# Reordered queues in a fused cross-attention and mixture-of-experts kernel: squares of K on ScalarE, scales ahead of low parts, gathers four blocks ahead

## The reference, cut to what matters

```python
# x: (4, 512, 512)   ctx: (4, 512, 256)
y = layernorm(x)
q = ln(y @ Wq + bq)                       # 16 heads of 32, normalised per head
k, v = ln(ctx_main @ Wk + bk), ctx_main @ Wv + bv          # 496 keys
k_dca, v_dca = split(ctx_dca @ Wkv_dca + bkv_dca)          # 16 keys, k_dca normalised too
x1 = x + (attn(q, k, v) + attn(q, k_dca, v_dca)) @ Wo + bo
h = layernorm(x1)
scores = softmax(h @ gate_w.T)            # 64 experts
top6 = top_k(scores, 6)                   # weights normalised to sum 1
# each expert takes at most 384 rows: gate, up (352 wide), silu, down
out = x1 + sum_of_top6(w_e * swiglu_e(h)) + swiglu_shared(h)   # shared one is 704 wide
```

## Time and profile before

| | us |
|---|---|
| median of three runs | 1766.02 (1765.25 to 1768.4) |
| the profiled execution | 1762.85 |
| its span | 1761.1 |
| TensorE busy in it | 1693.0 (96%) |
| VectorE, ScalarE, GpSimd busy | 1090.3, 1028.3, 757.9 |
| mean granted clock of TensorE | 0.982 |

### The profile page before, as it was taken

One profiled execution on the slowest core, in us unless ns is written; L12 is line 12 of the kernel. 1 busy time (PEld: TensorE's weight loads), 2 busy tenths in 40 slices (PEclk: granted clock), 3 DMA queues, 4 the chain that ended last, 5 costly groups with the idle time before them and its releaser, 6 DMA issues. The chain is left out here.

```text
span 1761.1 us, 35834 instructions
## 1 busy us (share of the span) xinstructions
PE 1693.0 (96%) x11782; PEld 1539.8 (87%) x11782; DVE 1090.3 (62%) x2157; ACT 1028.3 (58%) x1871; POOL 757.9 (43%) x719
## 2 busy tenths in 40 slices
PE   4899999999999999999999999999999999999995
PEld 3588888888888888989999999999999999999984
DVE  7555656777566665443666666666666666666664
ACT  4567766666545553222566666666666666666664
POOL 7513222334223230242245555555555555455554
PEclk8899999999899999999999999999999999999997
DMA  5543433433222532312577777777777777777766
GB/s 189 160 117 91 119 105 97 121 95 98 83 84 79 177 107 87 122 38 86 181 227 232 209 214 226 218 210 223 223 216 205 228 221 213 222 232 206 215 198 212
DMA packets 149083, 289.87 MB, mean 165 GB/s; under 512 B 29199, under 2 KB 66319, under 8 KB 139649
## 3 DMA queue, kind: packets, MB, share of 16 engines
q1 hardware_dynamic: 116112, 238.21, 41.9%
q0 software_dynamic: 32880, 50.51, 13.7%
HBM read 243.73 MB, written 64.52 MB: 175 GB/s over the span
## 5 line engine op out<-in xcount | busy, mean ns | idle before, releaser
L2188 POOL DMA_INDIRECT out<-y,ids_s x128 | 209.9, 1640 | 280.3 <-ACT y L2323 254.8
L2448 PE MATMUL ps<-xt_hi,gu_hi 128*128 128x256 f32 (+1 forms) x1856 | 303.5, 285 | 0.6 <-issue 0.6
L2448 PE MATMUL ps<-xt_lo,gu_hi 128*128 128x256 f32 (+1 forms) x1856 | 289.8, 278 | 0.0
L2448 PE MATMUL ps<-xt_hi,gu_lo 128*128 128x256 f32 (+1 forms) x1856 | 289.2, 278 | 0.0
L2223 DVE TENSOR_TENSOR gu_lo<-raw_gu,gu_hi 128x1408 fp32r<-128x1408 f32 (+2 forms) x132 | 214.6, 1625 | 112.5 <-ACT gu_hi L2220 109.3
L1121 ACT ACTIVATE prob<-ps 128x512 f32<-128x512 f32 x256 | 152.2, 597 | 191.4 <-PE ps L1428 169.6
L2448 PEld LDWEIGHTS ps<-xt_hi,gu_hi 128*128 128x128 f32 (+1 forms) x1856 | 250.6, 181 | 9.0 <-issue 3.0
L2448 PEld LDWEIGHTS ps<-xt_lo,gu_hi 128*128 128x128 f32 (+1 forms) x1856 | 244.4, 181 | 0.0
L2448 PEld LDWEIGHTS ps<-xt_hi,gu_lo 128*128 128x128 f32 (+1 forms) x1856 | 244.2, 181 | 0.0
L2168 POOL DMA_INDIRECT xg<-h_rows,ids_g x128 | 191.6, 1497 | 115.2 <-POOL ids_g L2163 50.6
L2280 ACT ACTIVATE h_hi<-h 128x256 fp32r<-128x256 f32 (+1 forms) x240 | 100.6, 419 | 224.0 <-DVE h L2349 223.4
(11 more groups left out here) (316 smaller groups left out, 3000.3 us busy)
## 6 DMA issues: line engine op xcount, KB each, us to landing
raw_gu<-in_w_gu SPq DMA_DIRECT2D x71, 1408.0 KB, 6.7
raw_d<-in_w_d SPq DMA_DIRECT2D x71, 512.0 KB
raw_d<-in_w_d SPq DMA_DIRECT2D x71, 192.0 KB
qs<-qk_rows SPq DMA_DIRECT2D x192, 64.0 KB, 2.2
ks<-qk_rows SPq DMA_DIRECT2D x192, 64.0 KB, 2.0
xa<-in_x SPq DMA_DIRECT2D x16, 256.0 KB, 3.0
qk_rows<-k_hi SPq DMA_DIRECT2D x16, 256.0 KB, 2.2
qk_rows<-k_lo SPq DMA_DIRECT2D x16, 256.0 KB, 2.5
```

What stands on the lines that cost most here:

```text
L2188: pool.indirect_dma_start(out=out, out_offset=bass.IndirectOffsetOnAxis(B.ids_s[:, p, k:k + 1], 0), in_=B.y[:, p, k, :], in_offset=None, b ...
L2448: last = pe.matmul(gu_banks(it, c)[half], gu_columns(w, it, half, d, c), x[:, x_p, d, 0:W], start=i == 0, stop=i == len(steps) - 1)
```

## The change

- Front, K's squares: ScalarE makes them in the front too, after `xt_high` (steps 1 to 3) or after `turned_full` of Q (steps 4, 5); GpSimd keeps Q's. The front of VectorE does `scales` and `ctx_rest` before `rest` of Q. The joined bias `bd` is done in two halves: the sum with `bv` stays at the beginning of step 3, the subtraction of means moves to its end (`bias_of_dca`), and the numbers of `POOL_SPLIT` follow. Tile 1's rows are turned, rounded and subtracted before tile 0's K product and biases.
- Heads: GpSimd counts after scaling; VectorE's `weighted(n)` before `route_top`, `route_mask` after `scales`, `route_code` into the fourth head before the second maxima, slots and weights after `weighted(n+2)`; TensorE turns K before `third_key` where there is a Q product in the unit, and otherwise after `route_pos`.
- Passage: TensorE weighs the last head first and spreads Wo's halves between the turned tiles; the cuts of the last tiles come before those of the first item.
- Experts: `scatter` copies its indices before it waits; after the last items, third blocks are gathered four ahead, their columns copied one block ahead; SyncE loads the gate and up weights of block b+3 and the down weights of block b+2; ScalarE's `act_d` comes before `results`.

The diff, without two hunks that only adapt final waits and the list of returned functions:

```diff
@@ -207,7 +207,7 @@
         SPLIT = dict(wq0=1, wq1=2, cols=3, wk=4, cd=5, kvd0=6, kvd1=7)
-        POOL_SPLIT = dict(bias=1, wv=2, wd_v=3, wd_k_centred=4, bd=5, wd_k=6, wo=6 + DC)
+        POOL_SPLIT = dict(bias=1, wv=2, wd_v=3, wd_k_centred=4, wd_k=5, bd=6, wo=6 + DC)
@@ -555,7 +555,6 @@
                     pool.tensor_tensor(bd[:, D:2 * D], bd[:, D:2 * D], bv[:], ALU.add)
-                    without_means(bd[:, 0:D].rearrange("p (g d) -> p g d", d=HD), sums_bd[:], H)
@@ -571,12 +570,14 @@
-            def squares(j, v, sq, given, summed, done, dca):
+            def bias_of_dca(s):
+                if s == 3:
+                    without_means(bd[:, 0:D].rearrange("p (g d) -> p g d", d=HD), sums_bd[:], H)
+
+            def squares(j, v, sq, given, summed, done):
                 if not tile(j):
...
                 pool.wait_ge(given.sem, given.value(j, 1))
-                if dca and j % T == T - 1:
-                    pool.wait_ge(kd_in.sem, kd_in.value(j // T, 16))
                 if j >= 1:
@@ -588,13 +589,13 @@
             def front(s):
-                squares(s - 2, kb, sq_k, k_bias, k_sum, k_sq, True)
                 weights_first(s)
...
                 weights_then(s)
-                squares(s - 1, qb, sq_q, q_bias, q_sum, q_sq, False)
+                squares(s - 1, qb, sq_q, q_bias, q_sum, q_sq)
                 k_rest(s - 2)
+                bias_of_dca(s)
@@ -620,9 +621,9 @@
-                counted_on(u - 6)
                 scaled(u + 5, kb, H, k_sum, kn_ready)
                 scaled(u + 5, qb, 0, q_sum, qn_ready)
+                counted_on(u - 6)
                 biased(u + 6, P, qb, bq, q_raw, q_bias)
@@ -913,17 +914,19 @@
                     summed(s - 2, sq_k, H, k_sq, k_sum)
+                    scales(s - 7)
+                    ctx_rest(s - 1)
                     if s < 6:
                         rest(s - 3, q_full, q_hi, q_lo, q_high, q_low, q_out)
-                    ctx_rest(s - 1)
-                    scales(s - 7)
                     front_dca(s)
                 j = s - 1
+                if s == 1:
+                    xt_rest(s, FX)
                 taken(j, P, qb, front_q(j), bq, q_ready, trq_ready, q_raw, q_bias)
                 taken(j, keys_of(j), kb, front_k(j), bk, k_ready, trk_ready, k_raw, k_bias)
-                if s < 6:
+                if 1 < s < 6:
                     xt_rest(s, FX)
-                else:
+                if s == 6:
                     summed(s - 1, sq_q, 0, q_sq, q_sum)
@@ -948,33 +951,33 @@
                 maxima(n + 2, 1)
+                weighted(n)
                 route_top(u - 6)
-                weighted(n)
-                route_mask(u - 6)
...
                 scales(u)
+                route_mask(u - 6)
                 maxima(n + 3, 1)
...
                 weighted(n + 1)
-                route_code(u - 6)
...
                 rest(u + 5, k_full, k_hi, k_lo, k_high, k_low, k_out)
+                route_code(u - 6)
+                maxima(n + 4, 1)
+                weighted(n + 2)
                 route_slots(u - 6)
-                maxima(n + 4, 1)
                 route_weights(u - 6)
-                weighted(n + 2)
                 summed(u + 6, sq_q, 0, q_sq, q_sum)
...
             weighted(HEADS - 1)
+            at_rest(WAIT1 + 1)
             residual(WAIT1)
+            at_rest(WAIT1 + 2)
             net.cut_x(dve, item, 0, False)
             net.cut_x(dve, item, 1, False)
-            at_rest(WAIT1 + 1)
-            at_rest(WAIT1 + 2)
             net.cut_gu(dve, item, 0, False)
@@ -1270,6 +1273,7 @@
                 normal(1)
+                xt_high(1, FX)
                 act.wait_ge(wv_in, WV_IN)
@@ -1280,7 +1284,7 @@
                 if s == 1:
-                    xt_high(1, FX)
+                    squares(0, kb, sq_k, k_bias, k_sum, k_sq, True)
                     return
@@ -1293,7 +1297,11 @@
                     xt_high(s, FX)
+                if s < 4:
+                    squares(s - 1, kb, sq_k, k_bias, k_sum, k_sq, True)
                 turned_full(s - 2, FQ_T, trq_ready, q_full, 0, False, q_low)
+                if 4 <= s < 6:
+                    squares(s - 1, kb, sq_k, k_bias, k_sum, k_sq, True)
                 if s == 2:
@@ -1347,10 +1355,10 @@
             item = net.item
+            at_high(WAIT1 + 1)
+            at_high(WAIT1 + 2)
             net.cut_x(act, item, 0, True)
             net.cut_x(act, item, 1, True)
-            at_high(WAIT1 + 1)
-            at_high(WAIT1 + 2)
             net.cut_gu(act, item, 0, True)
@@ -1666,10 +1674,13 @@
                     front_v(s - 3)
+                if s == 1:
+                    front_x(s)
                 if s < 6:
...
                     front_k_product(s - 1)
-                    front_x(s)
+                    if s > 1:
+                        front_x(s)
                     front_q_turned(s - 2)
@@ -1712,9 +1723,12 @@
                 half1(n + 2)
+                if tile(u + 6):
+                    k_turned(u + 5)
+                third_key(n + 2)
                 route_pos(u - 6)
-                k_turned(u + 5)
-                third_key(n + 2)
+                if not tile(u + 6):
+                    k_turned(u + 5)
                 fourth_key(n + 2)
@@ -1725,16 +1739,6 @@
-            item = net.item
-            pe.wait_ge(at_lo.sem, at_lo.value(WAIT1, 1))
-            pe.wait_ge(h2T_in.sem, h2T_in.value(WAIT1 - 1, 1))
-            wo_half(WAIT1, 0)
-            weigh(HEADS - 1, 0)
-            weigh(HEADS - 1, 1)
-            wo_half(WAIT1, 1)
-            weigh(HEADS - 1, 2)
-            weigh(HEADS - 1, 3)
-
             def a_last(j, free, use):
@@ -1746,12 +1750,19 @@
+            item = net.item
+            for t in range(T):
+                weigh(HEADS - 1, t)
+            pe.wait_ge(at_lo.sem, at_lo.value(WAIT1, 1))
+            pe.wait_ge(h2T_in.sem, h2T_in.value(WAIT1 - 1, 1))
+            wo_half(WAIT1, 0)
+            a_last(WAIT1 + 1, v_ready, TILES - 1)
+            wo_half(WAIT1, 1)
+            pe.wait_ge(nmT_in.sem, nmT_in.value(HEADS - 1, 1))
+            a_last(WAIT1 + 2, pos_taken, GROUP1 - 1)
             pe.wait_ge(nmax_ready.sem, nmax_ready.value(HEADS - 1, 2))
...
             net.transpose_chunk(pe, item, 1)
-            a_last(WAIT1 + 1, v_ready, TILES - 1)
-            pe.wait_ge(nmT_in.sem, nmT_in.value(HEADS - 1, 1))
-            a_last(WAIT1 + 2, pos_taken, GROUP1 - 1)
             wo_last(WAIT1 + 1, pv_taken, HEADS - 1)
@@ -2175,12 +2186,12 @@
         p = it.half
+        pool.tensor_copy(B.ids_s[:, p, 0:nb], slots_of(it, B.ids)).then_inc(s_copied.sem, 1)
         if it.known and it.e == SH_ITEMS:
...
             pool.wait_ge(added.sem, added.value(it.expert - 1, 16 * nb))
-        pool.tensor_copy(B.ids_s[:, p, 0:nb], slots_of(it, B.ids)).then_inc(s_copied.sem, 1)
         pool.wait_ge(y_taken.sem, y_taken.value(it.rows, nb))
@@ -2196,10 +2207,14 @@
                 thirds["gather_first"](pool, (it + 2).e - ITEMS)
+            if not (it + 1).exists:
+                thirds["gather_first"](pool, 2)
             scatter(pool, it - 1)
...
         def after(it):
-            thirds["gather_first"](pool, 2)
+            thirds["gather_first"](pool, 3)
+            thirds["weight_column"](pool, FIRST)
+            thirds["row_column"](pool, FIRST)
             scatter(pool, it)
@@ -2328,8 +2343,8 @@
             thirds["act_x"](act, FIRST + 1)
+            thirds["act_d"](act, FIRST)
             results(it)
-            thirds["act_d"](act, FIRST)
@@ -2606,24 +2621,28 @@
     def sync(sp):
-        def load(e, b, gu_done, d_done):
-            src = ins["w_d"][bass.ds(e, 1)].rearrange("a f n -> (a f) n")
-            sp.wait_ge(*gu_done)
+        def load_gu(b, done, turn):
+            e = expert(sp, b)
+            sp.wait_ge(done.sem, done.value(turn, 2))
             sp.dma_start(B.raw_gu[:, b.p].rearrange("p a n -> p (a n)"),
                          ins["w_gu"][bass.ds(e, 1)].rearrange("a p n -> p (a n)")).then_inc(gu_in[b.p].sem, 16)
-            sp.wait_ge(*d_done)
+
+        def load_d(b, done, turn):
+            e = expert(sp, b)
+            src = ins["w_d"][bass.ds(e, 1)].rearrange("a f n -> (a f) n")
+            sp.wait_ge(done.sem, done.value(turn, 1))
             sp.dma_start(B.raw_d[:, b.p, 0:2, :], src[0:2 * P, :].rearrange("(c p) n -> p c n", p=P)).then_inc(d_in[b.p].sem, 16)
...
         for k in range(2):
-            load(expert(sp, FIRST + k), FIRST + k, (S.gu_lo.sem, S.gu_lo.value(LAST_ITEM.weights - 1 + k, 2)),
-                 (S.d_lo.sem, S.d_lo.value(LAST_ITEM.weights - 1 + k, 1)))
-        load(expert(sp, FIRST + 2), FIRST + 2, (gu_lo.sem, gu_lo.value(0, 2)), (d_lo.sem, d_lo.value(0, 1)))
+            load_gu(FIRST + k, S.gu_lo, LAST_ITEM.weights - 1 + k)
+            load_d(FIRST + k, S.d_lo, LAST_ITEM.weights - 1 + k)
+        load_gu(FIRST + 2, gu_lo, 0)
         def body(b):
-            e = expert(sp, b + 3)
```

(25 more changed lines are left out.)

6 lines of the change are left out of this document (2 added, 4 removed).

## The result

The changed kernel is slower: 1775.6 us median (20 executions, 1764.1 to 1786.2) against 1764.6 (20 executions, 1754.2 to 1777.5), a ratio of 1.0060 with a 95% interval of 1.0042 to 1.0078. Forecast were 1755 and a range of 1747 to 1764. The profiled execution took 1784.5 us (span 1782.7), 21.6 us more than that of before.

What follows compares the result with a forecast made beforehand. TensorE was taken as the bound, fully busy in the experts, idle elsewhere, with a scatter chain setting the end. Terms of -5 -6.5 -0.85 -1.2 -3 -2 +4 +3.5 sum to -11.0 us: 1755.0 median, range 1747 to 1764.

Steps and rivals of the forecast that it cites:

- the count of the clock's falls: Heads: the old fall at half clock goes (6.5 us gained), one new one comes at unit edges (3.5 lost).
- (b): Heads: falls merely move; three more give 1765.5 us, two and a half 1763.7; chance 0.16 for two or more beyond the one.
- (c): Edges of units 6 to 9: waits for maxima plus four falls cost 30 against gains of 18.5: 1777; chance 0.05.
- Rival (a): Heads: the old fall goes and no new one comes; 1751.5 us, 1747.5 if the code block costs nothing; chance 0.25.
- Part 1: Front: K's squares on ScalarE and earlier scales give 5 us (2 to 8), K(1)'s turn near 42.5 us.
- rival (d): Front: squares on ScalarE need function table loads, taking back 6.4 us: 1761.4; chance 0.05.
- Part 2: Heads, units 6 to 9: maxima later behind the code block lose 4 us (0 to 5), one clock fall 3.5.
- Part 3: Heads, units 10 to 15: the `kb` wait (0.85 us) and its clock fall (6.5) go; `pv` waits give 1.2.
- Parts 4 and 5: Passage gives 3.0 us (1 to 3.6), some 0.6 waiting left; tail gives 2 (0 to 4), scatters still 8.4 apart.

Runs made afterwards that it cites:

- e4: Changed kernel with VectorE's scales in the front behind the low parts of Q and of the context again: 1766.0 us, ratio to before 1.0014.
- e6: Changed kernel with the code block ahead of the maxima of head n+4 again and the slots block in their middle: 1773.8 us, ratio to before 1.0045.
- e9: e7 with the slots and weights blocks behind the weighing of head n+2, no routing between the maxima of head n+4: 1755.1 us, ratio 0.9953.
- e2: Changed kernel with VectorE's whole order in the units of the heads as before the change: 1758.9 us, ratio to before 0.9979.
- e3: Changed kernel with the order of the heads' units on TensorE, VectorE and GpSimd as before: 1762.1 us, ratio to before 0.9995.
- e7: Changed kernel with VectorE's whole old order, in the units and in the front: 1752.7 us, ratio to before 0.9927.
- e15: e9 with two filling products on TensorE in unit 10 alone: 1751.1 us, ratio to before 0.9931.
- e16: e15 with three filling products in the passage, ahead of the last head's weighing: 1751.7 us, ratio to before 0.9927.
- e18: e15 with the last head's keys and queries loaded ahead of the second shared item's weights and rows: 1748.3 us, ratio to before 0.9903.
- e12: Kernel before with the order of the passage alone: 1764.5 us, ratio to before 1.0007.
- e11: Kernel before with the part on the routed experts and the tail alone: 1762.2 us, ratio to before 0.9997.
- e10: Changed kernel with the expert mask alone moved back ahead of the maxima of head n+3: 1809.4 us, ratio to before 1.0256.
- e14: e10 with four products of unused result on TensorE ahead of the wait in each of units 10 to 15: 1767.1 us, ratio to before 1.0026.

## Why the prediction was wrong

**The failed step is the count of the clock's falls.** It said: the old one goes (-6.5), one new one comes at the edges (+3.5), so -3 net. The profiled execution had three in the heads and the passage, worth 8.4, 8.5 and 16.1 us, 33 in all, so both the number and the price of one were too low; and all of the difference of the medians is clock. Rivals (b) and (c) named falls as the danger but put them at the edges of units 6 to 9. There the waits came, 1.18 to 1.42 us, and the clock stayed: in the eight traces with these waits (32 of them) one short stretch of 3.4 us follows one. Two of the falls were in units 12 and 13 and the third at the last head's keys; with the variants they are in all of the units 10 to 15, where TensorE has no product of Q or K left (and of V only in units 10 and 11), and where the prediction counted only gains. So the place of a wait mattered here more than its length. Why the place matters is read from the timelines alone: no run moved a wait and left it as long as it was.

Rival (a) also leaned on a wait "in the front after which the clock stayed". The trace of before has none of such length: behind or within each wait of 1.5 us and more between 20 and 90 us, after 2.08, 4.25, 1.89 and 1.81 us, the clock went to half, and the other two stood in time that was already at half. One of them, TensorE's row and a window behind it:

```profile
23.23 0.70 PE L1455 MATMUL ps<-wk_hi,cT_hi 128*128 128x512 f32 x2 [2.08 <-DVE wk_lo L841]
```
```profile
24.00:34.00 10.00, 7.88 (x20) 5.33 (x18) 7.46 (x11) 4.22 (x9) 8.86 (x6) 0.50 0.03 8
```

The 4.1 us of the earlier trace rows also count one of the front's (1.50 us at 85.22); the four edge waits of the heads are 2.6.

**Part 1, the front: wrong in size and sign.** Forecast -5, measured +2.4 (82.73 against 80.36). The collision of VectorE's low parts with GpSimd's scalings stood there as a reason for a smaller gain only. e4 shows the whole of the order at 4.8 us. In the step at 53 us the collision is 1.75 us of it; the low parts also stand behind the wait for the deviations and the scales, and the next rows of x come later through SyncE's queue. How the 4.8 us divide among the three was not tried. The rest of the front gives 2.4. K(1)'s turn was forecast at 42.5 and came at 43.6. No function table was loaded in the front: `Square` beside `Sqrt` is free here, so rival (d) is out. The Trainium skill, "GPSIMD Engine Reference", section "8. Key points", says that GpSimd and VectorE contend where a VectorE instruction has two SBUF inputs; the 1.32 and 1.53 us agree.

**Part 2: the mechanism right, its size less.** The edge waits grew from 0.84, 0.59, 0.59 and 0.60 us to 1.42, 1.19, 1.18 and 1.19, so 2.4 us against 4; undoing it gave 1.8 (e6), within the noise. e9 shows that the block between the two maxima is what they wait for: without it no such wait is left.

**Part 3.** The wait for `kb` and the fall at 444 us went, and so did the waits for `pv`, as said. Not seen: with `weighted(n)` first, TensorE no longer stops for VectorE and reaches the score bank while ScalarE is between its two table loads. The new wait is about as long as those it replaced (0.45 against 0.49 us; 0.67 in unit 10), but a fall followed within 2.5 us in 2 of 5 cases (with e4 and e6, 6 of 16), and after none of the 0.49 us waits for `pv` in the traces of before, e2, e3, e7, e9, e15, e16 and e18, one in each. Whether the place of the counting products adds to that was not separated.

**Parts 4 and 5.** Waits in the passage went from 3.9 to 1.8 us, forecast 0.6; the half clock behind the weighings took that back (e12), and the last head's keys became a wait that the prediction did not have. They land 9.5 to 10.4 us after their issue behind the shared experts' weights, its queries 11.1 to 11.8; in the kernel before the keys took 8.7 to 9.7 as well, and were there just in time for the product at 598.59 us. The tail's 2 us were not confirmed (e11). Its four scatters did move closer, 9.6, 7.4 and 5.9 us apart instead of 8.4, which the prediction had excluded; but in e12, with the old tail, they stand 7.2, 8.0 and 8.3 apart.

## What to carry to other kernels

Before moving work off a wait, look at the granted clock and at what TensorE does around that wait: a wait of a microsecond among the weighings of units 10 to 15 (128x33 and 128x66) was followed by 8 to 12 us lost here in 11 of 12 cases, while 31 of 32 waits of 1.2 to 1.4 us at the edges of units 6 to 9, ahead of products of 128x512, were not followed by half clock. Why the two places differ no run shows. Where such a wait cannot go, two useless products ahead of it are cheap: about half a microsecond. Compare medians of many executions together with their clocks: at equal clock the two kernels were alike, and that said at once where to look. One profiled execution can be the fastest or slowest of its kernel, so count stretches beside its time and the median.

## What was unexpected of the hardware

A single wait of 1.0 us in units 10 to 15 was followed by 17 to 24 us at 1.2 GHz eleven times of twelve; two waits of 0.5 and 0.4 us, 9.6 us apart (e7 at 500 and 510 us), were not. Filling them brought 42 us (e10 to e14) for 5.6 us of added products (four took 0.93 us). And the two-input operations of VectorE beside GpSimd's scaling lose nearly the same time whatever their size: 128x256 goes from 0.42 to 1.32 us, 128x512 from 0.68 to 1.53.
